# Dense attention part of a one-core transformer kernel: bias of v folded behind the output product, parts of q and k made by two engines, stack loads ordered by part, layer norm in halves

## The reference

```
xn = layernorm(x)
q = (xn @ Wq.T + bq)...; k = (xn @ Wk.T + bk)...; v = (xn @ Wv.T + bv)...   # 16 heads of 8
zq = q @ V;  zk = k @ V;  zv = v @ V
att = softmax(einsum('bhqr,bhkr->bhqk', zq, zk) / sqrt(32))
y = (einsum('bhqk,bhkr->bhqr', att, zv) @ U.T)...
dense = y @ Wo.T + bo
out = x + dense + six_layers(xn)
```

## Time and profile before

| what | value |
|---|---|
| median of 3 runs | 2557.55 us (2550.57 to 2572.85) |
| the profiled execution's own time | 2566.67 us |
| its span in the profile | 2564.8 us, so 1.9 us lie around it |
| busy share of the span | PE 87%, DVE 79%, ACT 69%, POOL 51% |
| mean granted TensorE clock | 0.928 of full |

### The profile page before, as it was taken

One profiled execution on the slowest core, in us unless ns is written; L12 is line 12 of the kernel. 1 busy time (PEld: TensorE's weight loads), 2 busy tenths in 40 slices (PEclk: granted clock), 3 DMA queues, 4 the chain that ended last, 5 costly groups with the idle time before them and its releaser, 6 DMA issues. The chain is left out here.

```text
span 2564.8 us, 82297 instructions
## 1 busy us (share of the span) xinstructions
PE 2224.1 (87%) x34487; PEld 1379.1 (54%) x34487; DVE 2038.6 (79%) x2417; ACT 1765.5 (69%) x4192; POOL 1307.7 (51%) x1085
## 2 busy tenths in 40 slices
PE   5899999999996788888888888888989888888986
PEld 3122222222223566676776767677767767667764
DVE  6999989989953878777877778787888788788873
ACT  1277878878774667776776767676777777677762
POOL 4111111111003667777776767666776667677750
PEclk8599999999998889999998989998999999999997
DMA  1213222312112322433233323423243323433321
GB/s 39 82 50 89 61 79 61 89 49 65 36 63 54 90 74 70 118 83 76 75 78 105 82 76 76 118 74 87 76 117 80 84 66 76 117 76 88 84 71 47
DMA packets 167464, 197.61 MB, mean 77 GB/s; under 512 B 87479, under 2 KB 105141, under 8 KB 167093
## 3 DMA queue, kind: packets, MB, share of 16 engines
q1 hardware_dynamic: 166740, 192.14, 28.4%
q10 hardware_dynamic: 352, 0.20, 0.1%
HBM read 57.83 MB, written 27.26 MB: 33 GB/s over the span
## 5 line engine op out<-in xcount | busy, mean ns | idle before, releaser
L699 ACT ACTIVATE PT<-E_ps 128x512 f32<-128x512 f32 x1024 | 534.4, 602 | 196.6 <-PE E_ps L1242 195.1
L938 DVE TENSOR_REDUCE mx<-S_ps 128x1 f32<-128x1024 f32 x512 | 601.5, 1218 | 37.1 <-PE S_ps L1233 31.4
L639 POOL TENSOR_TENSOR tc<-tc,ts 128x1024 f32<-128x1024 f32 x192 | 453.8, 2379 | 9.5 <-DVE ts L1012 9.3
L647 POOL TENSOR_TENSOR tc<-tc,rs 128x1024 f32<-128x1024 f32 x192 | 371.6, 1956 | 13.8
L1233 PE MATMUL S_ps<-KS,QS 48*128 48x512 bf16 x1024 | 330.7, 408 | 31.0 <-DVE mx L938 22.0
L601 POOL TENSOR_TENSOR pr<-pr,mxB 128x1024 f32<-128x1024 f32 x96 | 184.4, 1920 | 310.6 <-DVE mxB L1045 310.6
L1274 PE MATMUL B_ps<-w_qkv,x_cut 128*128 128x512 f32 x576 | 276.7, 480 | 68.4 <-DVE ts L1012 58.0
L1242 PE MATMUL E_ps<-QS,KS 64*128 64x512 bf16 x1024 | 321.8, 391 | 4.7 <-ACT PT L699 4.6
L762 ACT ACTIVATE pr<-B_ps,mxB 128x64 f32<-128x64 f32 x1536 | 324.0, 372 | 0.7 <-DVE mxB L1031 0.7
L581 POOL CAST w_cut_b<-w_raw_b 128x512 fp32r<-128x512 f32 (+1 forms) x48 | 27.6, 574 | 558.4 <-DMA w_raw_b<-in_Wqkv 418.1
L1337 PE MATMUL B_ps<-xy,vs 64*64 64x32 f32 x6144 | 217.7, 226 | 80.9 <-issue 73.1
(11 more groups left out here) (191 smaller groups left out, 4354.0 us busy)
## 6 DMA issues: line engine op xcount, KB each, us to landing
xy<-pc SPq DMA_DIRECT2D x768, 64.0 KB, 2.1
vs<-v SPq DMA_DIRECT2D x96, 384.0 KB, 3.6
Wqkv_cut<-w_cut_b SPq DMA_DIRECT2D x72, 256.0 KB, 2.4
w_qkv<-Wqkv_cut SPq DMA_DIRECT2D x36, 512.0 KB, 5.1
rot<-in_rot SPq DMA_DIRECT2D x96, 128.0 KB, 2.6
vs<-v SPq DMA_DIRECT2D x96, 128.0 KB, 3.7
w_raw_b<-in_Wqkv SPq DMA_DIRECT2D x36, 256.0 KB, 3.1
W_cut<-w_cut_b SPq DMA_DIRECT2D x24, 170.5 KB, 2.6
```

The costliest lines, as they stand in the source:

```text
L639: e.tensor_tensor(tc[:, :], tc[:, :], m.ts[i][:, :], ALU.add).then_inc(s[f"rot{n}"], 1)
L647: e.tensor_tensor(tc, tc, m.rs[u % 2][2][:, i * H:(i + 1) * H].unsqueeze(2).to_broadcast([P, H, DH]), ALU.mult).then_inc(s[f"{n}_scaled"], 1)
L699: e.activation(m.PT[n % NPT][:, :], turns.bank("probs", n)[:, :], ACT.Exp).then_inc(turns.sem("probs", n), 1)
L938: e.tensor_reduce(m.mx[h % 2][:, i, hf:hf + 1], m.S_ps[n % 2][:, :, :], AX.XY, ALU.max).then_inc(s["sc_max"], 1)
```

## The change

In the order of time:

1. SP loads x first, in two halves with a semaphore each; the layer norm goes by halves: DVE takes sum, mean and deviation of each half, ACT (not DVE) squares it, DVE sums the squares, and one operation (not two) makes the argument of the root. The last multiplication is two operations, and PE's first transposes wait for the first of them only.
2. The cast of the identity goes from DVE's beginning to behind the parts.
3. POOL no longer writes `ones_row`, and writes `va` behind the eight blocks of `QS` and `KS`.
4. The bias of v is no longer added to v. It is folded into a column (`bv_col`), multiplied by `w_out` in one small product, and added to `bo` by DVE. The 16 one-row products (L1221) are gone.
5. The first q product waits for the first chunk of `xn_T`, not for all four.
6. The middle part is made by ACT, not DVE; both engines run in a staggered order. `part` is replaced by `z_rest`, `z_mid`, `z_sub`, `z_low`.
7. v goes through the banks (5, 6, 7, 4); its last chunk waits for all eight remainders. PE waits for `va` at unit 2, not before unit 0.
8. SP issues all stack DMAs, those of head 0 for k too, and by part: high as soon as the high part is complete, then middle, then low.

```diff
+V_BANKS = (5, 6, 7, 4)
...
 def sync_a(e, w, m, s, d):
+    for i in range(2):
+        half = slice(i * NT // 2, (i + 1) * NT // 2)
+        e.dma_start(m.x_tok[:, half, :], m.x_rows[:, half, :]).then_inc(s[f"ld_x{i}"], 16)
...
-    e.dma_start(m.x_tok[:, :, :], m.x_rows).then_inc(s["ld_x"], 16)
...
-        w.wait_ge(s["part"], 4 * NC)
-        for r, (i, j) in enumerate(PAIRS):
...
+        for part, done in enumerate(("z_hi", "z_mid", "z_low")):
+            for n, to_stack, which in (("q", m.QS[sl], 0), ("k", m.KS[sl], 1)):
+                w.wait_ge(s[done], NC * (which + 1))
+                for r, pair in enumerate(PAIRS):
+                    if pair[which] == part:
+                        to = slice(base + r * HD, base + (r + 1) * HD)
+                        e.dma_start(to_stack[to, :], m.zp[n][rows_of(h), part, :]).then_inc(s[f"ld_stack{h % 4}"], 16)
...
 def gpsimd_a(e, w, m, s):
-    e.memset(m.ones_row[:, :], 1.0).then_inc(s["const"], 1)
...
-    e.memset(m.va[:, :, :, :], 1.0).then_inc(s["zeroA"], 1)
     for h in range(4):
...
+    w.wait_ge(s["zeroA"], 10)
+    e.memset(m.va[:, :, :, :], 1.0).then_inc(s["zeroA"], 1)
...
 def scalar_a(e, w, m, s, d):
+    for i in range(2):
+        half = slice(i * NT // 2, (i + 1) * NT // 2)
+        w.wait_ge(s["lnA"], 3 * (i + 1))
+        e.activation(m.sq[:, half, :], m.x_tok[:, half, :], ACT.Square).then_inc(s["sqA"], 1)
...
+    def middle_part(i, g):
+        n = "qk"[i]
+        w.wait_ge(s["z_rest"], NC * i + g + 1)
+        e.activation(m.zp[n][:, 1, chunk_cols(g)], m.z[n][:, chunk_cols(g)], ACT.Copy).then_inc(s["z_mid"], 1)
+
+    for k in range(2 * NC + 1):
+        if k < 2 * NC:
+            high_part(*divmod(k, NC))
+        if k:
+            middle_part(*divmod(k - 1, NC))
...
-    for r, (i, j) in enumerate(PAIRS):
-        e.dma_start(m.KS[0][r * HD:(r + 1) * HD, :], m.zp["k"][rows_of(0), j, :]).then_inc(s["ld_stack0"], 16)
...
 def vector_a(e, w, m, s):
-    w.wait_ge(s["ld_id"], 16)
-    e.tensor_copy(m.ident_bf[:, :], m.ident[:, :]).then_inc(s["idb"], 1)
...
+    for i, hf in enumerate(halves):
+        x = m.x_tok[:, hf, :]
+        w.wait_ge(s[f"ld_x{i}"], 16)
+        e.tensor_reduce(mean[:, hf], x, AX.X, ALU.add).then_inc(s["lnA"], 1)
+        w.wait_ge(s["lnA"], 3 * i + 1)
+        e.tensor_scalar(mean[:, hf], mean[:, hf], 1.0 / P, None, ALU.mult).then_inc(s["lnA"], 1)
+        w.wait_ge(s["lnA"], 3 * i + 2)
+        e.tensor_tensor(x, x, wide(mean[:, hf]), ALU.subtract).then_inc(s["lnA"], 1)
+    for i, hf in enumerate(halves):
+        w.wait_ge(s["sqA"], i + 1)
+        e.tensor_reduce(var[:, hf], m.sq[:, hf, :], AX.X, ALU.add).then_inc(s["lnA"], 1)
+    w.wait_ge(s["lnA"], 8)
+    e.tensor_scalar(c, var, 1.0 / P, 1e-5, ALU.mult, ALU.add).then_inc(s["rA_arg"], 1)
...
+    for i, hf in enumerate(halves):
+        e.tensor_tensor(m.sq[:, hf, :], m.x_tok[:, hf, :], wide(r[:, hf]), ALU.mult).then_inc(s["lnA"], 1)
...
+    w.wait_ge(s["fold_mm"], 9)
+    e.tensor_tensor(m.bo[:, :], m.bo[:, :], m.banks[0][:, 0:1], ALU.add).then_inc(s["fold"], 1)
...
+    for k in range(2 * NC + 1):
+        if k < 2 * NC:
+            high_rest(*divmod(k, NC))
+        if k:
+            low_part(*divmod(k - 1, NC))
+    w.wait_ge(s["ld_id"], 16)
+    e.tensor_copy(m.ident_bf[:, :], m.ident[:, :]).then_inc(s["idb"], 1)
...
 def tensor_a(e, w, m, s):
-    w.wait_ge(s["lnA"], 7)
     for g in range(NC):
+        w.wait_ge(s["lnA"], 9 + g // 2)
...
     w.wait_ge(s["fold"], 8)
-    w.wait_ge(s["xT"], NC)
+    e.matmul(m.banks[0][:, 0:1], m.w_out[:, :], m.bv_col[:, :], start=True, stop=True).then_inc(s["fold_mm"], 1)
...
+        bank = m.banks[V_BANKS[g]]
+        w.wait_ge(s["z_rest"], 2 * NC if g == NC - 1 else g + 1)
         for j in range(4):
...
-            mm = e.matmul(bank[:, c], m.ones_row[:, :], m.bv_row[:, :], start=False, stop=True, skip_group_check=True)
...
-    w.wait_ge(s["va"], NC)
...
+        if u == 2:
+            w.wait_ge(s["va"], NC)
```

More of the change, by code:

```diff
@@ L195, in memory @@
     m.ident, m.ident_bf = sb(ctx, "ident", [P, P]), sb(ctx, "ident_bf", [P, P], BF16)
-    m.ones, m.ones_row = sb(ctx, "ones", [P, P]), sb(ctx, "ones_row", [1, P])
+    m.ones = sb(ctx, "ones", [P, P])
     m.carry = sb(ctx, "carry", [P, 1])
@@ L209, in memory @@
         m.b_z = {n: sb(a, "bz_" + n, [P, 1]) for n in ("bq", "bk")}
-        m.bv_row, m.wo_T = sb(a, "bv_row", [1, P]), sb(a, "wo_T", [P, P])
+        m.bv_col, m.wo_T = sb(a, "bv_col", [P, 1]), sb(a, "wo_T", [P, P])
         m.z = {n: sb(a, "z_" + n, [P, T]) for n in "qk"}
@@ L332, in wait_part_a @@
     w.wait_ge(s["ld_o1"], 16 * NC * H)
-    w.wait_ge(s["part"], 8 * NC)
+    w.wait_ge(s["z_low"], 2 * NC)
     w.wait_ge(s["idb"], 1)
@@ L679, in scalar_a, with high_part @@
         e.activation(m.xn_T[:, chunk_cols(g)], m.banks[1 + g], ACT.Copy).then_inc(s["xT"], 1)
[L680 to L684, removed]
+    def high_part(i, g):
+        n = "qk"[i]
+        w.wait_ge(s["z_mm"], NC * i + g + 1)
+        e.activation(m.zp[n][:, 0, chunk_cols(g)], m.banks[(5 + NC * i + g) % 8], ACT.Identity,
+                     bias=m.b_z["b" + n][:, 0:1]).then_inc(s["z_hi"], 1)
+    def middle_part(i, g):
+        n = "qk"[i]
+        w.wait_ge(s["z_rest"], NC * i + g + 1)
[5 more added lines that the diff above has]
+            middle_part(*divmod(k - 1, NC))
     for g in range(NC):
         w.wait_ge(s["v_mm"], g + 1)
-        w.wait_ge(s["zeroA"], 3)
-        bank = m.banks[(5 + g) % 8]
+        w.wait_ge(s["zeroA"], 11)
+        bank = m.banks[V_BANKS[g]]
         e.activation(m.va[:, 4 * g:4 * g + 4, :, 0:HD], bank.rearrange("p (j h d) -> p j h d", j=4, h=H),
@@ L876, in vector_a @@
 def vector_a(e, w, m, s):
-    w.wait_ge(s["ld_id"], 16)
-    e.tensor_copy(m.ident_bf[:, :], m.ident[:, :]).then_inc(s["idb"], 1)
     mean, var = m.stat[:, 0, :], m.stat[:, 1, :]
     c, t, r = m.stat[:, 2, :], m.stat[:, 3, :], m.stat[:, 4, :]
[L881 to L895, removed]
+    halves = [slice(i * NT // 2, (i + 1) * NT // 2) for i in range(2)]
+    wide = lambda a: a.unsqueeze(2).to_broadcast([P, NT // 2, P])
+    for i, hf in enumerate(halves):
[11 more added lines that the diff above has]
+    e.tensor_scalar(c, var, 1.0 / P, 1e-5, ALU.mult, ALU.add).then_inc(s["rA_arg"], 1)
     w.wait_ge(s["rA_exp"], 1)
@@ L911, in vector_a @@
     w.wait_ge(s["fold_mm"], 6)
-    e.tensor_copy(m.bv_row[:, :], m.banks[6][0:1, 0:P]).then_inc(s["fold"], 1)
+    e.tensor_copy(m.bv_col[:, :], m.banks[6][:, 0:1]).then_inc(s["fold"], 1)
     w.wait_ge(s["fold_mm"], 7)
@@ L916, in vector_a, with high_rest, low_part @@
     e.tensor_copy(m.w_out[:, :], m.banks[0][:, 0:P]).then_inc(s["fold"], 1)
[L918 to L931, removed]
+    w.wait_ge(s["fold_mm"], 9)
+    e.tensor_tensor(m.bo[:, :], m.bo[:, :], m.banks[0][:, 0:1], ALU.add).then_inc(s["fold"], 1)
+    def high_rest(i, g):
+        n, c = "qk"[i], chunk_cols(g)
+        w.wait_ge(s["z_hi"], NC * i + g + 1)
+        e.scalar_tensor_tensor(out=m.z[n][:, c], in0=m.banks[(5 + NC * i + g) % 8], scalar=m.b_z["b" + n][:, 0:1],
+                               in1=m.zp[n][:, 0, c], op0=ALU.add, op1=ALU.subtract).then_inc(s["z_rest"], 1)
+    def low_part(i, g):
+        n, c = "qk"[i], chunk_cols(g)
+        w.wait_ge(s["z_mid"], NC * i + g + 1)
+        e.tensor_tensor(m.z[n][:, c], m.z[n][:, c], m.zp[n][:, 1, c], ALU.subtract).then_inc(s["z_sub"], 1)
+        w.wait_ge(s["z_sub"], NC * i + g + 1)
+        e.tensor_copy(m.zp[n][:, 2, c], m.z[n][:, c]).then_inc(s["z_low"], 1)
+    for k in range(2 * NC + 1):
[5 more added lines that the diff above has]
+    e.tensor_copy(m.ident_bf[:, :], m.ident[:, :]).then_inc(s["idb"], 1)
     turns = ExpTurns(m, s)
@@ L1193, in tensor_a @@
         e.matmul(m.banks[1 + i][:, 0:P], m.w_raw[n][:, :], m.bdV[:, :], start=True, stop=True).then_inc(s["fold_mm"], 1)
-    for i, n in enumerate(("bq", "bk")):
+    for i, n in enumerate(("bq", "bk", "bv")):
         e.matmul(m.banks[4 + i][:, 0:1], m.bdV[:, :], m.b_col[n][:, :], start=True, stop=True).then_inc(s["fold_mm"], 1)
-    e.matmul(m.banks[6][0:1, 0:P], m.b_col["bv"][:, :], m.bdV[:, :], start=True, stop=True).then_inc(s["fold_mm"], 1)
     w.wait_ge(s["ld_id"], 16)
@@ L1207, in tensor_a @@
     w.wait_ge(s["fold"], 8)
-    w.wait_ge(s["xT"], NC)
+    e.matmul(m.banks[0][:, 0:1], m.w_out[:, :], m.bv_col[:, :], start=True, stop=True).then_inc(s["fold_mm"], 1)
     for i, n in enumerate(("Wq", "Wk")):
         for g in range(NC):
-            if i:
-                w.wait_ge(s["xT"], g + 1)
+            w.wait_ge(s["xT"], g + 1)
+            if i == 0 and g == 3:
+                w.wait_ge(s["fold"], 9)
             e.matmul(m.banks[(5 + NC * i + g) % 8], m.w_z[n][:, :], m.xn_T[:, chunk_cols(g)], start=True, stop=True).then_inc(s["z_mm"], 1)
-    w.wait_ge(s["const"], 2)
     for g in range(NC):
-        w.wait_ge(s["part"], 4 * g + 1)
-        bank = m.banks[(5 + g) % 8]
+        bank = m.banks[V_BANKS[g]]
```

(7 more changed lines are left out.)

18 lines of the change are left out of this document (5 added, 13 removed).

## The result

The changed kernel takes 2545.35 us (median of 20 runs, 2524.64 to 2557.08), the kernel before 2560.8 in its 20 runs on the same chips: ratio 0.9926, 95% interval 0.9906 to 0.9947, so 14 to 24 us less. Forecast were 2541 and a change within 1%. The profiled execution took 2543.40 with a span of 2541.6.

The account below looks back on a forecast made before the run. Two bounds on the preparation, one behind the other: DVE's parts until 49.6, then v's products, ACT's copy and queue. Gain 17.6 (A) or 15.8 (B), less 0.3, middle 16.5: 2557.55 - 16.5 = 2541; range 2528 to 2556.

Parts of the forecast that it names:

- The handover: From the first score product on: its gain is handed on one for one to head 0 and all that follows.
- The layer norm: DVE at the start: small scalar operations on SBUF data wait for running memsets; root's argument done at 14.6 or 16.45.
- case A: Layer norm: root's argument slips in at the seventh block memset's end, done at 14.6; first score product at 44.75.
- B: Layer norm: root's argument waits for the eighth block memset, done at 16.45; first score product at 46.6.
- Folds: PE's output fold at 19.35 or 21.2; first high part 5.2 later, at 24.55 or 26.4.
- Parts: q and k parts: DVE's chunk falls from 2.31 to 1.85 and sets the pace; last low part 40.2, against 49.63.
- Stacks: SP's queue, the last wait: nine loads from 35.75, the ninth at 41.1; product 3.65 later, 2.5 as other bound.
- Contention: POOL's copies to `stream` beside DVE's first chunks: charged 0.3, with 0 and 1.2 as ends.
- The bias of v: v on PE: 16 of 32 products go, last chunk done by 41; without cover it would cost nothing until 44.75.
- The clock: Heads' ends: a longer interval, with TensorE at its lower level, costs 4.2; four of 14 were long.
- three short ones always follow a long one: Intervals between head ends (41.61 short, 45.84 long): a beat of its own that a shift leaves as frequent.
- The rivals on either side: Clock at heads' ends: more long intervals, loss over 1%, 6 in 100; fewer or better part B clock, 2528, 14 in 100.

Follow-up runs that it names:

- experiment 4: Changed kernel with POOL's long memset of `va` moved behind the fourth of the eight blocks; first score product at 48.98, 5.15 later.
- 11: Changed kernel with the layer norm whole again (one load, squares on DVE, two scalar operations), POOL's new order kept; first score product at 51.81, 8.0 later.
- experiment 1: Kernel before with only the bias of v moved behind the output product; first score product at 57.22, 5.2 earlier than before.
- experiment 7: Changed kernel with three unused identity products on PE in the pause at each head's end; median 2521.46 us, ratio 0.9858 to the kernel before.
- Experiment 2: Changed kernel with the bias of v back as 16 one-row products; first score product at 48.18, against 43.83 in the changed kernel.
- experiment 3: Changed kernel with the middle parts made by DVE again, ahead of each subtraction; first score product at 47.55, 3.7 later.

## Why the prediction was right

*The time.* 2541 was forecast from a gain of 16.5; the medians differ by 15.5, the ratio says 19, the first score product 18.55. Right in size and in mechanism. That 2545.35 lies above the forecast though the product gained more comes from the base: the forecast started from 2557.55, a median of three, and the kernel before has 2560.8 over its 20. The rest is scatter. The single terms below are off by up to 1.3, in both directions, and partly cancel.

*The handover.* Shown: 18.55 at the first score product are 18.5 at the end of head 0, and part B takes what it took, in these two profiles.

*The layer norm.* Argument at 14.6 in case A; measured 14.76. I had called A or B a toss-up and taken the middle; it was A each time, which is 0.9 of what the forecast lacks. The mechanism, a scalar operation that waits for a memset, was shown by experiments 4 and 11. The first half of x was there at 4.68, forecast near 5. What I weighed of the Trainium skill stands on two of its pages: the exclusion for a whole instruction in "SBUF — State Buffer", section "Who interferes with whom", and that data in PSUM can't enter such a mode in "VectorE: DVE Perf Modes", section "Mode 2×_2P — use both read ports for one tensor". The traces agree on both sides: 6.42 on eight elements in SBUF, and 0.28 for the fold copies from PSUM inside the 6.93 memset.

*Folds.* The output fold at 19.35, measured 19.33. The first high part at 24.55, measured 25.32, 0.8 late: PE's last transposes took 1.06 (before 0.60) and its four q instructions 2.52 (before 1.95).

*Parts.* DVE's chunk at 1.85, measured 1.72:

```profile
34.11 0.74 DVE L938 SCALAR_TENSOR_TENSOR z_k<-S_ps,bz_bk,zp_k 128x512 f32<-128x512 f32 x1
...
35.83 0.74 DVE L938 SCALAR_TENSOR_TENSOR z_k<-S_ps,bz_bk,zp_k 128x512 f32<-128x512 f32 x1
```

From the remainder to DVE's next operation it is 0.66 here and was 0.78 before. In the staggered order that operation is the subtraction of the chunk before, which needs nothing from this remainder; I had not counted that. Last low part 40.2, measured 40.42.

*Stacks.* Nine loads back to back from 35.75, measured from 36.12. From the last issue to the product I took the 3.65 of before, and named 2.5 as the other bound; it is 2.37. That term was mis-sized by 1.3, and it is the largest error in the sum. Where SP alone issues it is 2.3 to 2.4 in all eleven profiles; where ACT issues too it was 3.65 before and 2.9 in experiment 1. That two queues at once are the reason is likely, but no run changes that alone. Contention was charged at 0.3, and that is what it cost: from the first remainder to the last low part it takes 14.38, and 14.07 in experiment 4, where POOL's copies are all but over when DVE begins. It varies, and is 0.7 in experiment 7 (14.77).

*The bias of v.* The step that was wrong, though it changed nothing in the sum: I said that v had room until 44.75 and did not ask what the bias rows were worth in the new order. Experiment 2 says 4.35, or 5.5 from PE's first v product.

*The clock.* The price of a long interval, 4.2, was right (4.3), and so was the place. My argument for its frequency, that three short ones always follow a long one, fell: the changed kernel has three and eight between its long ones, experiment 3 has one in 14. The rivals on either side stayed out. The pause behind them is worth about as much as the change by the ratios (17 us against 19, give or take 10 and 5) and less by the profiles (2.6 long intervals at 4.3 are 11, against 18.55).

## What to carry to other kernels

Where a kernel is one chain, find the first instruction of the steady work and ask what its last wait is, then what the next would be; here v, the parts and the issue queue lay one behind the other: the bias of v alone gave 5.2 of 18.55, and taking one of the others back cost 3.7 (the middle parts) or 5.4 (the order of the loads). Let casts and small scalar operations on SBUF data not fall beside a long GpSimd memset, or reckon when they will. And look at the short pauses of TensorE before a stretch at the lower clock: a few products that are thrown away, put where the engine waits anyway, took off a further 11 to 17.

## What had not been expected of the hardware

A product of 128x128 in f32 costs PE 0.22 when its like follow it (0.89 for a chunk of four in experiment 1), but 0.415 when one-row products alternate with it, and each of those costs as much: a chunk goes from 0.89 to 3.3 at full clock, to 5.8 at the lower level. In experiment 2 the granted clock fell at about 36.4 and was 0.52 on average over 36 to 48, a stretch in which PE has a product on record throughout, with such rows in between. The next stack load of eight rows follows 0.67 after the last on SP where SP issues alone, and a pause of PE of some 0.8, at the end of a head, comes ahead of a stretch at the lower level in 23 of 126 cases, and in none of 56 when 0.94 of work lies in it; why in those 23 stays open.
